# Moving the batches' norms and the softmax's reciprocal diagonals to POOL

## The reference

```python
x = x + jnp.tanh(g_xattn[0]) * _L0_xattn_ref(_layernorm(x), fside_BxS2xS2_0, ctx_1024)
x = x + jnp.tanh(g_ffn[0])   * _L0_ffn_ref(_layernorm(x), gate_w, gate_b, val_w, val_b, out_w, out_b)
x = x + jnp.tanh(g_xattn[1]) * _L1_xattn_ref(_layernorm(x), ctx_1024, Wq, bq, Wk, bk)
x = x + jnp.tanh(g_ffn[1])   * _L1_ffn_ref(_layernorm(x), router_w, down_w, up_w)

_layernorm(x) = (x - mean) / sqrt(var + 1e-5)
# first block: smooth-quantised linear, silu(gate) * up, a second smooth-quantised linear
# third block: attention = softmax(query @ key.T), x_m = x @ attention.T
```

## Time and profile before

| | |
|---|---|
| three runs | 481.84, 483.37, 484.09 us; median 483.37 |
| profiled execution | 481.64 us; span 479.5 us |
| busy in the span | PE 88%, DVE 80%, ACT 74%, POOL 47% |
| head, 0 to 214 us | PE 163.5, DVE 169.7, ACT 166.1, POOL 132.7 us busy |
| loop, 214 us to the end | PE 256.9, DVE 215.0, ACT 186.4, POOL 93.0 us busy |

### The profile page before, as it was taken

The page is one execution under the profiler, slowest core; times in us unless marked ns, Lnnn a source line. Parts: engine busy times, 40 slices in busy tenths (PEclk is TensorE's granted clock), DMA queues, the critical chain, the costliest instruction groups (busy, mean ns, idle before and its releaser), DMA issues.

```text
span 479.5 us, 6973 instructions
## 1 busy us (share of the span) xinstructions
PE 420.4 (88%) x1975; PEld 225.6 (47%) x1975; DVE 384.7 (80%) x969; ACT 352.5 (74%) x586; POOL 225.7 (47%) x333
## 2 busy tenths in 40 slices
PE   0586888968888987889999999999999999999976
PEld 0354645526435533345445545554554455455433
DVE  4878799997697688677898889889888988987642
ACT  1488888785879998967887778788777877876220
POOL 2281695785798775354333343433343333332121
PEclk9967799998999999999999999999999999999997
DMA  8999476175189321411221331223132212313201
GB/s 299 322 391 321 144 264 168 24 218 111 23 305 113 109 57 23 88 23 34 45 57 40 60 76 36 55 67 77 23 67 66 46 44 68 78 23 55 66 25 43
DMA packets 85879, 49.77 MB, mean 104 GB/s; under 512 B 72008, under 2 KB 74312, under 8 KB 84816
## 3 DMA queue, kind: packets, MB, share of 16 engines
q1 hardware_dynamic: 85840, 49.32, 39.3%
HBM read 28.33 MB, written 4.19 MB: 68 GB/s over the span
## 4 chain that ended last, share of the span: by engine, by line
PE 56%; DVE 13%; POOL 8%; issue 8%; ACT 6%; DMA 5%; SPq 2%; DVEq 0%; POOLq 0%; ACTq 0%
PE p_out L1733 10%; PE p_out L1768 10%; PE p_gate L1726 9%; PE p_val L1726 9%; PE p_out L1743 3%; PE p_tr L1708 3%; DVE rowmax L789 2%; PE p_out L1755 2%; DMA att_t<-in_L_ffn_val_w 2%; DMA w_in<-in_fside_BxS2xS 2%; SPq L401 1%; DVE h_max L749 1%; PE p_gate L1759 1%; PE p_tr L1620 1%; ACT val_t L1202 1%
## 5 line engine op out<-in xcount | busy, mean ns | idle before, releaser
L1726 PE MATMUL p_val<-val_t,q_room 128*128 128x512 fp8e4 x256 | 65.7, 379 | 0.6 <-ACT p_val L1336 0.5
L1726 PE MATMUL p_gate<-gate_t,q_room 128*128 128x512 fp8e4 x256 | 65.7, 379 | 0.2 <-ACT p_gate L1326 0.2
L1733 PE MATMUL p_out<-att_t,qT_room 128*128 128x512 f32 x128 | 58.9, 602 | 1.6 <-ACT qT_room L1164 1.6
L1768 PE MATMUL p_out<-out_t,ws_f 128*128 128x512 fp8e4 x256 | 58.5, 379 | 0.6 <-DMA ws_f<-ws_f 0.4
L570 POOL TENSOR_TENSOR rstd<-mv,ln_eps 128x1 f32<-128x1 f32 x48 | 9.2, 192 | 94.9 <-DVE mv L841 94.9
L1326 ACT ACTIVATE p_gate<-w_slots,seed_scale 128x512 f32<-128x512 f32 x64 | 43.6, 683 | 10.5 <-POOL seed_scale L587 9.2
L1311 ACT ACTIVATE ctx_sb<-p_gate,bcol 128x512 f32<-128x512 f32 x64 | 43.7, 683 | 8.5 <-issue 4.5
L868 DVE TENSOR_TENSOR act_f<-p_val,ctx_sb 128x512 f32<-128x512 f32 x64 | 44.1, 689 | 6.7 <-PE p_val L1726 5.0
L870 DVE TENSOR_REDUCE mu<-act_f 128x1 f32<-128x512 f32 x64 | 43.9, 686 | 2.2
L1336 ACT ACTIVATE p_val<-w_in,seed_scale 128x512 f32<-128x512 f32 x64 | 43.5, 680 | 0.0
L593 POOL TENSOR_TENSOR x_all<-x_all,q_room 128x512 f32<-128x512 f32 x16 | 20.3, 1270 | 41.9 <-ACT q_room L1265 39.0
(11 more groups left out here) (211 smaller groups left out, 965.6 us busy)
## 6 DMA issues: line engine op xcount, KB each, us to landing
att_t<-in_L_ffn_out_w SPq DMA_DIRECT2D x6, 1024.0 KB, 5.6
att_t<-in_L_ffn_gate_w SPq DMA_DIRECT2D x4, 1024.0 KB, 13.1
w_in<-in_fside_BxS2xS SPq DMA_DIRECT2D x4, 1024.0 KB, 7.0
att_t<-in_L_ffn_val_w SPq DMA_DIRECT2D x4, 1024.0 KB, 9.4
out_dram<-x_all SPq DMA_DIRECT2D x16, 256.0 KB, 2.3
x_all<-in_x SPq DMA_DIRECT2D x2, 1024.0 KB, 8.3
x_all<-in_x SPq DMA_DIRECT2D x1, 2048.0 KB, 12.6
ctx_sb<-in_ctx SPq DMA_DIRECT2D x4, 512.0 KB, 5.1
```

The lines of the kernel that those rows point to most:

```text
L1726: last = nc.tensor.matmul(bank[:, c % 2, :], x_t[n % 2][:, k * P:(k + 1) * P], w_t[m][:, k, cols], start=False, stop=k == KD - 1, skip_gro ...
L1733: last = nc.tensor.matmul(p_out[:, 0, :], lt_c[:, k * P:(k + 1) * P], att_t[:, bass.ds((n // T) * (KD * S) + k * S, S)], start=k == 0, sto ...
L1768: last = nc.tensor.matmul(p_out[:, 0, :], p_t[:, k * P:(k + 1) * P], w_t[2][:, k, :], start=k == 0, stop=k == KH - 1)
```

## The change

`h_normalise(b)` goes from DVE to POOL. There it adds a negated mean, so `h_reciprocal_deviation(b)` makes one: a new instruction subtracts the mean from zero into `ln_less`, with a buffer of zeros that one more memset fills. `t_normalise(b, t)` goes from ACT to POOL as a product of the identity with the broadcast reciprocal. What each waits for is as before. In POOL's list they are put at the places shown; the lists of DVE and ACT lose them and are otherwise as they were, PE's and SP's don't change.

```diff
@@ -146,6 +146,7 @@
         ln_rstd = sb("ln_rstd", [P, T], F32)
+        ln_less, ln_zero = sb("ln_less", [P, T], F32), sb("ln_zero", [P, T], F32)
         h_max = sb("h_max", [P, 2, KD], F32)
@@ -477,13 +478,14 @@
                     nc.gpsimd.memset(zeros[:, :], 0.0).then_inc(consts_made, 1)
+                    nc.gpsimd.memset(ln_zero[:, :], 0.0).then_inc(consts_made, 1)
                     nc.gpsimd.memset(ones[:, :], 1.0).then_inc(consts_made, 1)
...
                                             pattern=[[-1, E], [1, E]], channel_multiplier=0).then_inc(consts_made, 1)
-                    pool.wait_ge(consts_made, 11)
+                    pool.wait_ge(consts_made, 12)
 
@@ -499,9 +501,18 @@
                     need(pool, a_act, T * b)
-                    link = Chain(pool, a_pool_chain, b)
+                    link = Chain(pool, a_pool_chain, 2 * b)
+                    link(nc.gpsimd.tensor_tensor(ln_less[:, :], ln_zero[:, :], ln_mv[:, :, 0], ALU.subtract))
                     link(nc.gpsimd.tensor_tensor(ln_rstd[:, :], ln_mv[:, :, 1], ln_eps[:, :], ALU.add))
                     nc.gpsimd.tensor_tensor(ln_rstd[:, :], ln_rstd[:, :], half_neg[:, :], ALU.pow).then_inc(a_rstd, 1)
+
+                def h_normalise(b):
+                    pool.wait_ge(a_rstd, b + 1)
+                    need(pool, a_q16[0], T * (2 * b - 1))
+                    for t in range(T):
+                        cols = slice(t * D, (t + 1) * D)
+                        nc.gpsimd.tensor_scalar(act_f[:, cols], batch_of(b)[:, cols], ln_less[:, t:t + 1],
+                                                ln_rstd[:, t:t + 1], ALU.add, ALU.mult).then_inc(a_act, 1)
 
@@ -558,6 +569,11 @@
 
+                def t_normalise(b, t):
+                    pool.wait_ge(t_rz, 2 * b + t // 2 + 1)
+                    need(pool, t_probT, T * b + t - 1)
+                    nc.gpsimd.tensor_tensor(rz_diag[:, t % 2, :], ident[:, :], rz_att[:, t:t + 1].to_broadcast([P, P]), ALU.mult).then_inc(t_prob, 1)
+
                 def o_add(b, t):
@@ -606,6 +622,7 @@
                 h_reciprocal_deviation(0)
+                h_normalise(0)
                 root(0, 0)
@@ -613,6 +630,7 @@
                 scale_diagonal(0, 0)
+                h_normalise(1)
                 w_round(4)
@@ -627,9 +645,14 @@
                 smooth_diagonals(1, 0)
+                h_normalise(2)
+                t_normalise(0, 0)
                 o_scaled_act(0)
+                t_normalise(0, 1)
                 scaled_weights(1, 0)
                 h_reciprocal_deviation(3)
+                t_normalise(0, 2)
+                t_normalise(0, 3)
                 root(0, 2)
@@ -643,10 +666,15 @@
                 scale_diagonal(0, 2)
+                t_normalise(1, 0)
+                t_normalise(1, 1)
                 root(1, 1)
                 smooth_diagonals(1, 1)
+                h_normalise(3)
                 o_scaled_act(1)
                 scaled_weights(1, 1)
+                t_normalise(1, 2)
+                t_normalise(1, 3)
                 scale_diagonal(1, 1)
@@ -660,12 +688,16 @@
                 h_hidden(2, 2)
+                t_normalise(2, 0)
+                t_normalise(2, 1)
                 h_hidden(2, 3)
...
                 q_root(0)
+                t_normalise(2, 2)
                 o_scaled_act(2)
+                t_normalise(2, 3)
                 scaled_weights(1, 2)
@@ -684,12 +716,16 @@
                 smooth_diagonals(1, 3)
+                t_normalise(3, 0)
+                t_normalise(3, 1)
                 o_scaled_act(3)
...
                 o_add(3, 0)
+                t_normalise(3, 2)
+                t_normalise(3, 3)
                 c_root(0)
@@ -734,14 +770,6 @@
                     last.then_inc(a_stats, 1)
-
-                def h_normalise(b):
-                    dve.wait_ge(a_rstd, b + 1)
-                    need(dve, a_q16[0], T * (2 * b - 1))
-                    for t in range(T):
-                        cols = slice(t * D, (t + 1) * D)
-                        nc.vector.tensor_scalar(act_f[:, cols], batch_of(b)[:, cols], ln_mv[:, t, 0:1],
-                                                ln_rstd[:, t:t + 1], ALU.subtract, ALU.mult).then_inc(a_act, 1)
 
@@ -963,10 +991,9 @@
                 link0, link1 = Chain(dve, b_chain, 0), Chain(dve, b_chain, HC + 3)
-                dve.wait_ge(consts_made, 11)
+                dve.wait_ge(consts_made, 12)
                 h_statistics(0)
                 w_sum(0, 0)
-                h_normalise(0)
                 column_max(0, 0, 1, 0)
@@ -984,7 +1011,6 @@
                 w_sum(1, 0)
-                h_normalise(1)
                 column_max(0, 1, 1, 0)
@@ -1016,7 +1042,6 @@
                 column_max(0, 2, 1, 2)
-                h_normalise(2)
                 column_max(0, 2, 1, 3)
@@ -1053,7 +1078,6 @@
                 column_max(0, 3, 1, 1)
-                h_normalise(3)
                 column_max(0, 3, 1, 2)
@@ -1247,17 +1271,12 @@
 
-                def t_normalise(b, t):
-                    act.wait_ge(t_rz, 2 * b + t // 2 + 1)
-                    need(act, t_probT, T * b + t - 1)
-                    nc.scalar.activation(rz_diag[:, t % 2, :], ident[:, :], ACT.Copy, scale=rz_att[:, t:t + 1]).then_inc(t_prob, 1)
-
                 def t_transposed(b, t):
...
                 def silu_loaded():
-                    act.wait_ge(consts_made, 11)
+                    act.wait_ge(consts_made, 12)
                     nc.scalar.activation(silu_table[:, :], zeros[:, 0:1], ACT.Silu).then_inc(silu_table_loaded, 1)
@@ -1783,7 +1786,7 @@
 
-                pe.wait_ge(consts_made, 11)
+                pe.wait_ge(consts_made, 12)
                 columns(0, 0, 1, 0)
```

More of the change, by code:

```diff
@@ L1402, in _ @@
                 smooth_rows(1, 0)
-                t_normalise(0, 0)
-                t_normalise(0, 1)
                 tanh_gates()
@@ L1410, in _ @@
                 t_exponential(0, 3)
-                t_normalise(0, 2)
-                t_normalise(0, 3)
                 rounded(1, 0, 0)
@@ L1428, in _ @@
                 w_sum(2, 3)
-                t_normalise(1, 0)
-                t_normalise(1, 1)
                 rounded(0, 2, 1)
@@ L1436, in _ @@
                 t_exponential(1, 3)
-                t_normalise(1, 2)
-                t_normalise(1, 3)
                 t_transposed(1, 2)
@@ L1457, in _ @@
                 scale_row(0, 3)
-                t_normalise(2, 0)
-                t_normalise(2, 1)
                 rounded(0, 3, 1)
@@ L1466, in _ @@
                 smooth_rows(1, 2)
-                t_normalise(2, 2)
                 q_norm(0)
-                t_normalise(2, 3)
                 w_transposed(11)
@@ L1500, in _ @@
                 q_norm(2)
-                t_normalise(3, 0)
-                t_normalise(3, 1)
                 smooth_rows(1, 3)
@@ L1523, in _ @@
                 t_exponential(3, 3)
-                t_normalise(3, 2)
                 b_gate(1, 3)
-                t_normalise(3, 3)
                 t_transposed(3, 2)
```

## The result

| | median | runs | profiled execution |
|---|---|---|---|
| before | 483.38 us | 6 (481.84 to 484.09) | 481.64 us, span 479.5 |
| after | 488.89 us | 6 (487.57 to 491.52) | 488.81 us, span 486.9 |

The ratio of after to before is 1.0128, with a 95% interval of 1.0098 to 1.0158. The changed kernel is slower by 5.5 us by the medians and by 6.2 by the ratio; 488.0 was forecast, with 484.5 to 493.3 as the range. The profiled execution of before lies 1.7 us under its median and that of after at its own, so the two profiles are further apart, 7.4 us by their spans, than the kernels are.

What follows compares the result with a forecast made beforehand. The chain of waits between engines ahead of the tile loop, with POOL in it, was taken to bound the edit's effect. Losses of 1.7 + 2.0 + 0.9 = 4.6 us, set against the median 483.37, gave 488.0 us; range 484.5 to 493.3.

Steps and rivals of the forecast that it cites:

- Batch 0: First batch's softmax, beside norm(2): norm and diagonal (0,1) behind o_scaled_act(0) on POOL delay PE's second transpose; 1.7 us lost.
- The prices: Costs on POOL: four norms 2.8 us (bounds 2.24 to 4.96), a diagonal 0.40 us, a negation 0.28 us.
- Rival (a): Norms on POOL cost as much as two-input operations, 4.96 us for four, giving 492.3 us; chance 0.13.
- Batch 1: Second batch's softmax, beside norm(3): root, norm and diagonals on POOL delay the third weight's total; 2.0 us more lost.
- root(1,1): POOL's root in the second batch's softmax, behind diagonals (1,0) and (1,1), which take 0.8 us; loses 0.3 us.
- norm(3): Last batch's norm, near 114 us, on POOL ahead of o_scaled_act(1) and scaled_weights(1,1); charged 0.7 us.
- the diagonals (1,2) and (1,3): On POOL behind scaled_weights(1,1), ready at 124.8 and 125.2, delaying PE's second transpose; charged 1.0 us.
- Batch 2: Third batch's softmax: diagonals (2,0) and (2,1) between the hidden tiles cost 0.8 us, (2,3) at most 0.1; 0.9 us in all.
- norm(0) and norm(1): Norms of the first two batches, at 11 and 40 us: finished before PE wants them, so nothing lost or gained.
- (b): Batch 1's delay is absorbed by room around 120 to 130 us; only 1.7 us carry on, 485.1 us; chance 0.19.
- (c): Faster: DVE bounds the first half and loses 1.9 us of work twice, giving 479.6 us; chance 0.08.
- (d): POOL and DVE block each other: two more meetings of 1.0 us beside POOL work, giving 490.0 us; chance 0.10.

Runs made afterwards that it cites:

- the whole change on the base: The full diff of the change applied to the kernel before with plain DMAs for the transposing ones: 484.56 us median, ratio 1.0020 to the kernel before.
- the base: The kernel before with its 128 transposing DMAs replaced by plain DMAs of the same bytes: 478.53 us median, ratio 0.9915; an earlier single execution 481.07 us.
- diagonals alone: Only the sixteen diagonals moved to POOL, norms left on DVE, against the kernel with plain DMAs: 482.04 us median, ratio 1.0004 to the kernel before.
- norms alone: Only the four norms and the negation moved to POOL, diagonals left on ACT, against the kernel with plain DMAs: 479.34 us median, ratio 0.9924 to the kernel before.

## Why the prediction was right

**Batch 0: right.** 1.7 us were forecast, the traces show 1.96 in after and 1.96 in the whole change on the base, where two profiles of the base differ by 0.02. PE's gap ahead of the second transpose was to be some 1.3 us with POOL as releaser; it is 1.19 in both. The diagonals alone show 2.06, the norms alone 0.33. The forecast had the norm and the diagonal in one sum; the larger part of it is the diagonal behind `o_scaled_act(0)`.

**The prices: right.** A norm is 770 ns, where 700 was read off the row of 1024 elements; four take 3.02 us, for 2.8, within the bounds. A diagonal is 402 ns for 400. The negation takes 0.27 to 0.30 us, start to start, for 0.28. Rival (a), over 1.1 us a norm, is refuted. The estimate of 0.44 us plus dispatch that the prediction took from the Trainium skill (GPSIMD Engine Reference, Elementwise section) is further off. The same section also has some 1.8 cycles an element for a tight unrolled loop, 768 ns for 512 elements, and the 770 ns measured here are close to that figure; no run shows which loop the norm takes. By the prediction's own terms 0.44 for 0.70 us in two times four norms is 2.1 us less before any dispatch, where it said 1.5.

**Batch 1: one term was mis-sized.** The 2.0 us were 0.3 for root(1,1), 0.7 for norm(3) and 1.0 for the diagonals (1,2) and (1,3). The diagonals are right: PE's wait for them is 0.92 us in after, 0.92 in the whole change on the base, 0.91 with the diagonals alone. The root is nearly so. DVE's wait for it, after and then before:

```profile
118.57 0.17 DVE L800 TENSOR_SCALAR cm<-cm 128x2 f32<-128x2 f32 x1 [1.00 <-POOL cm L520]
```

```profile
113.00 0.17 DVE L772 TENSOR_SCALAR cm<-cm 128x2 f32<-128x2 f32 x1 [0.82 <-POOL cm L509]
```

That is 0.2 us on the spot, and over the whole stretch nothing is left of it (-0.06 and 0.01); but the stretch also has PE waiting for a load of `w_in`, 3.16 us before and 3.59 after, so it doesn't isolate the root. norm(3) is the term that was off. Its working took from the profile of before that `o_scaled_act(1)` is ready 2.06 us behind the smoothing diagonals. POOL's timeline in after:

```profile
120.19 3.03 POOL L514 TENSOR_SCALAR act_f<-x_all,ln_less,ln_rstd 128x512 f32<-128x512 f32 x4
123.85 2.50 POOL L569 TENSOR_TENSOR a_f<-a_f,o_rows 128x512 f32<-128x512 f32 x2 [0.63 <-ACT o_rows L1188]
126.31 2.49 POOL L551 TENSOR_TENSOR ws_o<-ctx_sb,o_rows 128x512 f32<-128x512 f32 x2
128.76 0.76 POOL L575 TENSOR_TENSOR rz_diag<-ident,rz_att 128x128 f32<-128x128 f32 x2
```

The norms end at 123.2, and `o_scaled_act(1)` waits 0.63 us more, for a row of ACT that waits for PE. So norm(3) set nothing in after, nor in the two variants that move the norms. POOL's idle time at this place is 2.06 us in before (from 113.44 + 1.19 to 116.69) and 1.96 with the diagonals alone, where PE has the products ahead of the rows at full clock; it is 3.73 and 3.90 us in the base's two profiles, where they are under the low clock. The norms need 3.02. By this, an estimate is that they would cost 1.0 us at full clock, near the 0.7 forecast; no profile with the norms on POOL has full clock here, so that isn't shown. The step that failed was to take this room from one profile as fixed: it depends on when PE makes the rows, and that goes with PE's clock.

After's stretch nevertheless grew by 2.65 us, 1.73 more than the diagonals' 0.92. That is what a slower PE takes, as the table of the seven profiles has it. These are rows of PE's timeline in after, where the softmax's first two tiles of batch 1 are transposed, then the second two, then the total:

```profile
117.58 3.78 PE L1694 MATMUL p_val<-rz_diag,e_att 128*128 128x128 f32 x16 [1.33 <-POOL rz_diag L575]
...
129.22 2.05 PE L1694 MATMUL p_val<-rz_diag,e_att 128*128 128x128 f32 x16 [0.92 <-POOL rz_diag L575]
132.05 0.36 PE L1583 MATMUL p_val<-abs_sum,ones 128*128 128x4 f32 x2 [0.78 <-ACT att_t L1188]
```

Sixteen products of one shape take 3.78 us at 117.58 and 2.05 at 129.22. The busy time by stretch gives the clock (length; in this order the busy time of PE, PEld, DVE, ACT, POOL; granted clock; DMA share; GB/s), first of after, then of before:

```profile
112.00:116.00 4.00, 2.56 (x16) 2.40 (x16) 2.45 (x4) 4.00 (x8) 2.49 (x3) 0.80 1.29 238
116.00:120.00 4.00, 2.67 (x13) 2.43 (x12) 2.73 (x10) 0.86 (x2) 2.40 (x5) 0.50 0.64 146
```

```profile
108.00:111.00 3.00, 2.85 (x14) 2.45 (x12) 1.20 (x5) 0.64 (x2) 1.04 (x1) 0.50 1.04 234
...
116.00:120.00 4.00, 3.49 (x21) 2.25 (x20) 3.81 (x7) 2.11 (x5) 3.31 (x3) 1.00 0.37 76
```

From 116 to 120 PE is at its lower level, 1.2 GHz, in after, and at 2.4 GHz in before, which had its low stretch earlier, around 108 to 111. In the 4 us ahead of 116, where after's clock fell, PE had been busy 2.56 of 4.00 us. The base has the low level under these products without the change, and PE's pause ahead of them is much the same, 1.33 us for POOL's diagonal in after and 1.29 for ACT's in before. So the 1.7 us are not shown to be the change's. Whether the change makes this place of the fall likelier, seven profiles can't tell.

**Batch 2: right.** 0.9 were forecast; 0.72 and 0.28 in after, 0.82 and 0.44 on the base. As the prediction said, PE's columns wait behind the two diagonals. norm(0) and norm(1), forecast as hidden, weren't tried apart; all norms together cost 0.4 to 0.8 us by the runs and 0.35 by the five middle stretches.

**What the forecast didn't have.** Two of the prediction's signs came out otherwise: the total of the third weight at 132.05 for 127.5, and the start of the loop 9.2 us late for 4.6. Of the 9.2, 1.73 are the low clock of batch 1, and 3.68 lie ahead of all that was charged: that late are the smoothing diagonals (1,0) in after. A part of it is a load. DVE's statistics of the second batch wait for their rows of x, after and then before:

```profile
28.08 2.47 DVE L767 BATCH_NORM_STATS2 ln_stats<-x_all 128x6 f32<-128x512 f32 x4 [3.01 <-DMA x_all<-in_x]
```

```profile
27.20 2.47 DVE L731 BATCH_NORM_STATS2 ln_stats<-x_all 128x6 f32<-128x512 f32 x4 [2.07 <-DMA x_all<-in_x]
```

Another is PE's clock. These are the same eight products in after, in before and in the base's first profile:

```profile
69.91 5.40 PE L1680 MATMUL p_val<-ctx_room,wqk_t 128*128 128x512 f32 x8 [0.74 <-ACT ctx_room L1188]
```

```profile
67.75 3.70 PE L1677 MATMUL p_val<-ctx_room,wqk_t 128*128 128x512 f32 x8 [0.74 <-ACT ctx_room L1164]
```

```profile
69.03 5.40 PE L1676 MATMUL p_val<-ctx_room,wqk_t 128*128 128x512 f32 x8 [0.74 <-ACT ctx_room L1163]
```

The granted clock from 70 to 74 us is 0.57 in after and 1.00 in before. From the start of these products to the smoothing diagonals (1,0) it is 10.27 us in after and 10.28 in the base's first profile, against 8.75 in before and 8.71 to 8.98 in the other four. So 1.5 of the 3.68 us are the low clock, and it comes without the change too. The other 2.16 are there before these products; they start earlier in before than in any other profile here (68.65 to 70.14). The whole change on the base is 0.68 us late at (1,0), the norms alone 0.72 early, and two profiles of the base differ by 1.08. So most of the 3.68 is those two executions' scatter, though with one profile of after the 2.16 aren't shown to be. At the other end it is the reverse, after and then before:

```profile
458.00:474.00 16.00, 12.87 (x54) 6.31 (x53) 7.81 (x32) 3.43 (x7) 4.53 (x10) 1.00 0.13 33
```

```profile
458.00:474.00 16.00, 12.92 (x37) 6.35 (x38) 6.52 (x25) 2.44 (x5) 2.66 (x4) 0.79 0.10 34
```

From the first spread to the end before took 270.3 us, after 268.5, the base 268.4 in both profiles, and the variants 268.2 to 269.7. The profile of before had the low clock in its tail and after's had not, which gives back 1.8 of the 7.4 us. The prediction's test, a loop unchanged in length, holds for the loop's tiles, 16.7 us each in both, and not for its last ones.

**The rivals.** (b), that batch 1's delay is absorbed: norm(3) was, a third of it, and the rest not. (c), faster: no; DVE's freed time went to idling. Its deciding point was a second transpose before 83.2, or some 86.9 with after's early 3.7 us; it came at 87.61. (d), the lock: DVE's small rows at their group, after and then before:

```profile
L819 DVE TENSOR_SCALAR scale<-rowmax 128x4 f32<-128x4 f32 x16 | 6.0, 377 | 0.6
```

```profile
L791 DVE TENSOR_SCALAR scale<-rowmax 128x4 f32<-128x4 f32 x16 | 5.1, 316 | 0.6
```

The mean rises from 316 to 377 ns, 0.9 us over sixteen. It is 319 and 343 in the base's two profiles, 374 with the norms alone, 400 with the diagonals alone. The meetings seem to become more frequent, and the Trainium skill's lock (SBUF — State Buffer, Who interferes with whom) agrees in kind. That taking 16 norms from DVE would also ease the lock, as the prediction worked out from that page, isn't seen: with the norms alone moved, and so taken away, the mean is higher than in the base. But the norms alone have nearly the whole rise and cost 0.4 to 0.8 us: the lock is a small part at most.

**What stays open.** The five stretches between the smoothing diagonals (1,0) and the first spread give 4.15 us for the profile pair on the base (1.96 + 0.01 + 0.92 + 0.82 + 0.44), where both have the low clock at like places, and 3.8 for after against before, once the 1.7 of the clock are taken off. The prediction's 4.6 without its 0.7 for norm(3) is 3.9. But the runs differ by 5.1 to 6.0 on the base and by 5.5 on the kernel itself. So that 488.0 lies so near to 488.89 is in part luck: norm(3) was charged and did not come, and another 1 to 2 us came that were not charged. On the base they are 0.68 us in the first stretch, within its scatter, and 1.3 in the loop, where the granted clock from 458 to 474 us is 0.88 with the change and 1.00 in the base; the kernel before has 0.79 there without the change. Over the timed executions the granted clock averages 0.968 with the whole change (eleven) and 0.971 in the base (six). Among the 28 executions of the kernel before, 0.010 more clock goes with 2.3 us less time, by which an estimate for the difference is 0.8 us; it isn't clear of the scatter of such averages. I can't assign the rest. Not tried: the diagonal (0,1) ahead of `o_scaled_act(0)`, which should close the gap of 1.19 us if the place is the cause; norms carried out twice; the norms of batches 0 and 1 only; each batch's diagonals alone; the change profiled a second time. So that the order makes the loss rests on the two halves of the change and on PE's gaps, not on a reordered list. No version faster than the kernel before came out of it.

## What to carry to other kernels

An engine's idle share says nothing of where in its list an instruction will stand. Before work goes to the idlest engine, read who waits for it and what stands ahead of it there: sixteen diagonals of the same price on both engines cost 3.5 to 4.3 us, sixteen norms that are 43% dearer 0.4 to 0.8. And before a term is charged for an engine's work, check in more than one profile how long it idles at that point for somebody else, and compare only profiles whose clock fell at like places.

## What the hardware showed unexpectedly

- PE's granted clock falls to the lower level at different places of the head from one execution to the next. At one place of the program sixteen 128x128 f32 products took 2.70 and 3.78 us in two executions of the base, and 2.05 in the kernel before. The time on to the total differed by only 0.17 us between the two of the base, since the one with the shorter products was slow in the two rows behind them (1.91 and 1.25 us against 1.18 and 1.03); against the kernel before both lost 1.7 to 1.8. The granted clock of the whole span was 0.965 and 0.964 in the base and 0.964 in after, so the mean doesn't show it; the stretch does.
- A one-input TENSOR_SCALAR of 128x512 f32 with two scalars from memory takes 770 ns on POOL, 1.43 times what it takes on DVE (540), and 1122 for 1024 elements into f16.
- A VectorE operation on four elements of each partition can take 0.97 us while POOL is at work, as at 139.28 before; the same row is in after:

```profile
147.50 0.97 DVE L819 TENSOR_SCALAR scale<-rowmax 128x4 f32<-128x4 f32 x1
```
